# Attention scores in single banks: one exponential per tile of keys, and a fourth side bank

## The chip, the cores and the metric

One core of a Trainium2 chip runs the whole program in one launch. The metric is the device time of one execution in microseconds (us). The core's engines each work through their own list of instructions in order: PE (matmul, with PEld for its weight loads), ACT (activations), DVE (vector), POOL (general purpose) and SP (issues DMAs). They meet through semaphores. PE writes to a memory of its own, PS in the code, with eight banks; a bank holds 512 fp32 numbers for each of 128 partitions.

## The reference

Two sublayers over x of 2 x 2048 tokens x 256, each modulated by a small conditioning vector c. What matters here is the attention of the second one:

```python
nx = _rmsnorm(X, g1)
Q = (nx @ Wq.T).reshape(B, S, H, dk).transpose(0, 2, 1, 3)     # H = 4, dk = 64, S = 2048
Kc = nx @ Wkc.T
Vc = nx @ Wvc.T
scores = jnp.einsum('bhsd,btd->bhst', Q, Kc) * scale
attn = jax.nn.softmax(scores, axis=-1)
out = jnp.einsum('bhst,btd->bhsd', attn, Vc)
```

Before it stand a layer norm, a projection and a softmax over heads; after it an output projection, routing of each token to 2 of 8 experts, the experts and a shared expert (gated feed-forward), and the combination.

## The kernel before

The program has three parts: FRONT (everything up to the queries, keys and values), the attention loop, and a tail with the experts. Each engine runs `run(work, todo)` over lists of named jobs, which were laid out by hand (FRONT) or by rules that spread them evenly (`loop_order`, `tail_order`); a job does on each engine what that engine has to do in it, and on the others nothing.

**The attention loop** has 256 steps, gs = 0 to 255. A step is one of 8 (batch, head) pairs bh, one of 4 blocks of 512 queries qb, and one of 8 pairs of key tiles kp (2 x 128 keys). Eight steps make a block. Four things are done for each step, on different engines and at different times:

- `qk(gs)` on PE: four matmuls of 512 columns, two tiles of keys, each with a high part (KA, L1748) and a low part (KB, L1751) that are added up in the same bank. They fill two neighbouring banks, 0 and 1 or 2 and 3 in turn.
- `exp(gs)` on ACT: one exponential over both banks, 128x1024, into PT (L777), then a rounded copy PH (L780). PT, PH and PL have four slots.
- `low(gs)` on DVE: PL = PT - PH (L1190), the part that rounding lost.
- `av(gs, n)` on PE: for each of the two tiles of keys three matmuls into bank 4 (L1766, L1767, L1768), which add up over the 16 tiles of a block. After the block's last one `o_out` on ACT copies bank 4 out to OZ (L789), and the first product of the next block waits for that copy (semaphore "o"). POOL then takes OZ through a chain of small DMAs to get the reciprocal of the sums.

Each step's time is cut into parts 0, 1 and 2 (and part 3, which stands before part 0 and is used only in the last step of a bh). On PE step gs issues the scores of step gs + 1 and the products of step gs - 2:

```python
for part in range(3):
    if part == 0 and gs + 1 < NGS:
        run(work, LOOP[gs, 3])
        qk(gs + 1)
    if part and gs >= 2:
        av(gs - 2, part - 1)
    run(work, LOOP[gs, part])
```

ACT runs `exp(gs + 1)` in part 0 and `o_out(gs - 2)` at the start of part 2. DVE runs `low(gs)` between parts 0 and 1.

**Side jobs** fill the parts. The largest is `max_mm`: row maxima for the softmax of a later block need their own scores, 512 matmuls of 128x512 on PE (L1716), each reduced on DVE (L1161), 16 per block. `q_mm` (L1702) makes queries of later heads, with copies on ACT (`qst`, L760, and L768) and DVE (`q_lo`). `nx_turn`, `k_mm` and `v_mm` make the other batch's keys and values, `proj` (L1729) is the output projection, `norm` and `norm_root` (L797, L803) are for the later router, and the last 32 steps hold routing and scatter for the experts. Every side job that writes PS takes the next bank of a ring, in the order of the program: `banks.add(job, [5, 6, 7])`. `bank(...)` makes PE wait until the job that last held this bank has been read out, by ACT or by DVE.

Of the kernel before, what the change touches and what calls it, by code (L numbers as in the profile page):

```python
# [6 lines left out]
ACT = mybir.ActivationFunctionType  # L7
# [5 lines left out]
P = 128  # L13
# [11 lines left out]
NSTEP = 32  # L25
NGS = 8 * NSTEP
# [224 lines left out]
def run(work, todo):  # L251
    for name, *args in todo:
        if name in work:
            work[name](*args)
# [8 lines left out]
def _build(nc, ctx, I, out):  # L263
    named = {}

    def sem(name):
        if name not in named:
            named[name] = ctx.enter_context(nc.semaphore(name))
        return named[name]

    def sb(name, shape, dt=F32, c=None):
        return (c or ctx).enter_context(nc.sbuf_tensor(name, shape, dt))
# [3 lines left out]
    PS = ctx.enter_context(nc.psum_tensor("PS", [P, 8, 512], F32))  # L276
# [115 lines left out]
    with ExitStack() as c:  # L392
        PT = sb("PT", [P, 4, 1024], c=c)
# [7 lines left out]
    QA = [Q01[0][:, :], Q01[1][:, :], QA2[:, :]]  # L401
    QB = [Q01[2][:, :], Q01[3][:, :], QB2[:, :]]
    KA, KB = [KA0[:, :], KA1[:, :]], [KB0[:, :], KB1[:, :]]
# [22 lines left out]
    banks = Banks()  # L426
# [3 lines left out]
    for gs in range(NGS):  # L430
        for part in (3, 0, 1, 2):
            for job in LOOP[gs, part]:
                banks.add(job, [5, 6, 7])
    loop = dict(banks.count, pe=banks.n)
    banks.turn = 0
    for s in range(-2, NTL + 3):
# [8 lines left out]
    def pe_of(w, key):  # L445

        w.wait_ge(sem("pe_use"), banks.pe[key])

    def front_done(w):
        w.wait_ge(sem("pe_use"), front["pe"])  # L450
        w.wait_ge(sem("act_out"), front["a"])
        w.wait_ge(sem("dve_out"), front["v"])
        w.wait_ge(sem("h2"), 8)
        w.wait_ge(sem("x2"), 8)
        w.wait_ge(sem("ql"), 8)
        w.wait_ge(sem("qd"), 8)
        w.wait_ge(sem("kb"), 4)
        w.wait_ge(sem("xp"), 8)
        w.wait_ge(sem("dotg"), 16)
        w.wait_ge(sem("d_spill0"), 16)  # L460
        w.wait_ge(sem("d_spill1"), 16)
        w.wait_ge(sem("d_gbs"), 16)
# [10 lines left out]

    def experts_free(w):

        w.wait_ge(sem("qk"), NGS)

    def q_free(w, bh):
        if bh < 2:
            pe_of(w, ("oproj", 1, 7, 0))  # L480
        elif bh == 2:
            front_done(w)
        else:
            w.wait_ge(sem("qk"), NSTEP * (bh - 2))

    def k_free(w, b):
        if b == 0:
# [21 lines left out]

    def keys_free(w):  # L510

        w.wait_ge(sem("qk"), 4 * NSTEP)
        pe_of(w, ("max_mm", 3, 3, 3, 3, 0))

    def scattered(b, r):
# [131 lines left out]
    def _(act):  # L647
        w = Once(act)
# [119 lines left out]
                act.activation(QA[bh % 3][r, cols], qst[r, :], ACT.Copy).then_inc(sem("qh"), 1)  # L768

        def exp(gs):  # L770
            bk = 2 * (gs % 2)
            w.wait_ge(sem("qk"), gs + 1)
            if gs == 0:
                front_done(w)
            if gs >= 4:
                w.wait_ge(sem("av"), 2 * (gs - 3))
            act.activation(PT[:, gs % 4, :], PS[:, bk:bk + 2, :].rearrange("p a n -> p (a n)"), ACT.Exp,  # L777
                           scale=0.125).then_inc(sem("pt"), 1)
            w.wait_ge(sem("pt"), gs + 1)
            act.activation(PH[:, gs % 4, :], PT[:, gs % 4, :], ACT.Copy).then_inc(sem("pt_h"), 1)  # L780

        def o_out(gs):
# [802 lines left out]
    def _(pe):  # L1585
        w = Once(pe)
# [119 lines left out]
        def q_dup(bh, c):  # L1706

            w.wait_ge(sem("qd"), 8 * (bh // 2) + 2 * c + bh % 2 + 1)
# [20 lines left out]
            pe.matmul(PS[:, k, 0:256], O[:, i * P:i * P + P], woa[:, pair % 2, :], start=True,  # L1729
                      stop=True).then_inc(sem("pe_use"), 1)  # L1730

        def qk(gs):

            bh, i = divmod(gs, NSTEP)
            b, qs = bh // 4, bh % 3
            qb, kp = divmod(i, 8)
            bk, qcols = 2 * (gs % 2), slice(qb * 512, qb * 512 + 512)
            w.wait_ge(sem("d_m"), 16 * (4 * bh + qb + 1))
            q_dup(bh, qb)
            w.wait_ge(sem("ql"), 8 * (bh // 2) + 2 * qb + bh % 2 + 1)  # L1740
            out_of(w, ("k_mm", b, kp // 2, 0))
            w.wait_ge(sem("kb"), 4 * b + kp // 2 + 1)
            w.wait_ge(sem("neg"), b + 1)
            if gs >= 2:
                w.wait_ge(sem("pt"), gs - 1)
            for n in range(2):
                k0 = (2 * kp + n) * P
                pe.matmul(PS[:, bk + n, :], KA[b][:, k0:k0 + P], QA[qs][:, qcols], start=True, stop=False)  # L1748
            for n in range(2):
                k0 = (2 * kp + n) * P  # L1750
                mm = pe.matmul(PS[:, bk + n, :], KB[b][0:65, k0:k0 + P], QB[qs][0:65, qcols], start=False, stop=True)  # L1751
            mm.then_inc(sem("qk"), 1)

        def av(gs, n):

# [97 lines left out]
                "rl_turn": rl_turn, "rl_mm": rl_mm, "count": count}  # L1853
        run(work, FRONT)
        front_done(w)
        qk(0)
        for gs in range(NGS):
            for part in range(3):
                if part == 0 and gs + 1 < NGS:
                    run(work, LOOP[gs, 3])  # L1860
                    qk(gs + 1)
                if part and gs >= 2:
                    av(gs - 2, part - 1)
                run(work, LOOP[gs, part])
        for gs in range(NGS - 2, NGS):
            av(gs, 0)
            av(gs, 1)
        w.wait_ge(sem("pt"), NGS)
        w.wait_ge(sem("o"), 32)
        w.wait_ge(sem("act_out"), loop["a"])  # L1870
        w.wait_ge(sem("dve_out"), loop["v"])
# [53 lines left out]
```

## Time and profile before

| | |
|---|---|
| time, median of 3 runs | 1437.05 us (1436.15 to 1437.35) |
| the profiled execution: its own time | 1436.41 us |
| its span in the profile | 1434.5 us |
| PE busy | 1270.5 us (89% of the span) |
| DVE busy | 1089.7 us (76%) |
| ACT busy | 892.1 us (62%) |
| the stretch of the attention loop that the rows below look at | 257 to 1036 us of the span; its last steps end near 1075 us |

The profile's page gives busy times, the span in 40 slices, the chain of waits and the costliest groups of instructions. A matmul's row shows about 0.4 us, but matmuls overlap in the pipeline: where PE does not wait, the next one of 512 columns starts 0.23 us after the last. So PE counts as busy also in pauses that are shorter than the overlap, and order and spacing have to be read from the timeline.

### The profile page before, as it was taken

The numbers are of one execution on the slowest core, as the hardware profiler recorded it, in microseconds if no ns is written. First come the engines' busy times: TensorE is split into PE (matmuls) and PEld (weight loads), VectorE is DVE, ScalarE is ACT, GpSimd is POOL, SyncE is SP. The second block draws the span as 40 slices with busy tenths as digits, with TensorE's granted clock in tenths as the row PEclk, the third lists the DMA queues.
The fourth block names the chain that finished last, engine by engine and source line by source line (L and its number), as shares of the span: only waits on it lengthen the run. The fifth ranks groups of instructions, "written<-read, shape, count | busy, mean of one in ns | idle before, by whom it ended". The sixth has DMA issues, their size and how long they took to land.

```text
span 1434.5 us, 18743 instructions
## 1 busy us (share of the span) xinstructions
PE 1270.5 (89%) x5896; PEld 905.9 (63%) x5896; DVE 1089.7 (76%) x2076; ACT 892.1 (62%) x1450; POOL 350.4 (24%) x381
## 2 busy tenths in 40 slices
PE   4777676899999999999998999999877799999994
PEld 2334544566666666676765666766545687887783
DVE  4957877687988877888878888888833757547688
ACT  2355565577776766776787766676636656555451
POOL 0443340112211121110212211111272001723346
PEclk9889787899999999999999999999979899999998
DMA  5000017100000000000000001000020423655644
GB/s 199 8 1 37 23 59 242 56 8 6 4 9 4 5 9 4 5 9 4 9 4 4 9 4 56 9 5 28 22 84 27 145 63 106 200 155 171 184 128 147
DMA packets 61376, 80.71 MB, mean 56 GB/s; under 512 B 12002, under 2 KB 51682, under 8 KB 61026
## 3 DMA queue, kind: packets, MB, share of 16 engines
q1 hardware_dynamic: 36384, 46.81, 10.1%
q0 software_dynamic: 10752, 21.18, 5.4%
q10 hardware_dynamic: 14146, 11.52, 2.4%
q8 instruction: 52, 0.85, 0.3%
q14 instruction: 42, 0.34, 0.1%
HBM read 41.79 MB, written 37.62 MB: 55 GB/s over the span
## 4 chain that ended last, share of the span: by engine, by line
PE 57%; DVE 10%; POOL 5%; DMA 4%; ACT 3%; issue 3%; SPq 2%; POOLq 0%; ACTq 0%; DVEq 0%
PE PS L1819 8%; PE PS L1748 7%; PE PS L1751 7%; PE PS L1766 6%; PE PS L1768 6%; PE PS L1767 6%; PE PS L1716 6%; PE PS L1845 4%; DVE mx L1161 4%; DVE PL L1190 3%; POOL xbuf L1540 2%; SPq L633 2%; POOL y L1552 2%; PE PS L1803 1%; PE PS L1702 1%
## 5 line engine op out<-in xcount | busy, mean ns | idle before, releaser
L777 ACT ACTIVATE PT<-PS 128x1024 f32<-128x1024 f32 x256 | 262.4, 1025 | 211.0 <-PE PS L1751 210.8
L1161 DVE TENSOR_REDUCE mx<-PS 128x1 f32<-128x512 f32 x512 | 336.9, 683 | 67.2 <-PE PS L1716 66.1
L1190 DVE TENSOR_TENSOR PL<-PT,PH 128x1024 fp32r<-128x1024 f32 x256 | 317.8, 1242 | 13.2 <-ACT PH L780 12.8
L780 ACT ACTIVATE PH<-PT 128x1024 fp32r<-128x1024 f32 x256 | 271.6, 1061 | 8.1
L1766 PE MATMUL PS<-PH,VH 128*65 128x512 f32 x512 | 215.1, 420 | 10.6 <-DVE PL L1190 8.8
L1768 PE MATMUL PS<-PL,VH 128*65 128x512 f32 x512 | 205.0, 400 | 0.0
L1767 PE MATMUL PS<-PH,VL 128*65 128x512 f32 x512 | 204.4, 399 | 0.0
L1716 PE MATMUL PS<-KA,Q 128*128 128x512 f32 x384 | 156.5, 418 | 9.6 <-DVE mx L1161 6.0
L1748 PE MATMUL PS<-Q,KA 128*128 128x512 f32 x384 | 129.2, 418 | 13.0 <-DMA Q<-mT 11.1
L1751 PE MATMUL PS<-Q,KB 65*128 65x512 f32 x384 | 123.0, 402 | 0.0
L1515 POOL DMA_DIRECT2D z_scratch<-OZ x32 | 17.6, 550 | 386.5 <-ACT OZ L789 386.5
L1716 PEld LDWEIGHTS PS<-KA,Q 128*128 128x128 f32 x384 | 74.7, 195 | 49.9 <-DVE mx L1161 15.9
L1767 PEld LDWEIGHTS PS<-PH,VL 128*65 128x65 f32 x512 | 70.7, 138 | 50.0 <-issue 5.4
L1768 PEld LDWEIGHTS PS<-PL,VH 128*65 128x65 f32 x512 | 70.5, 138 | 50.2 <-issue 2.4
L1540 POOL DMA_INDIRECT xbuf<-nxT,slot x64 | 65.0, 1015 | 141.5 <-DVE nxT L1348 123.8
L1766 PEld LDWEIGHTS PS<-PH,VH 128*65 128x65 f32 x512 | 70.8, 138 | 41.3 <-issue 16.3
L1370 DVE TENSOR_TENSOR xl<-PS,xh 128x256 fp32r<-128x256 f32 x110 | 46.3, 421 | 60.0 <-ACT xh L860 59.6
L1748 PEld LDWEIGHTS PS<-Q,KA 128*128 128x128 f32 x384 | 70.7, 193 | 33.3 <-DMA Q<-mT 11.5
L1552 POOL DMA_INDIRECT y<-ybuf,slot x64 | 62.3, 973 | 99.3 <-DVE X L1402 52.5
L1751 PEld LDWEIGHTS PS<-Q,KB 65*128 65x128 f32 x384 | 74.0, 193 | 17.9
L867 ACT ACTIVATE sg<-PS 128x256 f32<-128x256 f32 x110 | 42.2, 383 | 61.0 <-PE PS L1819 60.6
L1377 DVE TENSOR_TENSOR hg<-PS,sg 128x256 f32<-128x256 f32 x110 | 46.3, 421 | 41.8 <-ACT sg L867 41.7
(243 smaller groups left out, 2502.6 us busy)
## 6 DMA issues: line engine op xcount, KB each, us to landing
xbuf<-xT SPq DMA_DIRECT2D x26, 384.0 KB, 4.9
xg<-xbuf SPq DMA_DIRECT2D x78, 128.0 KB, 2.3
ybuf<-yo ACTq DMA_DIRECT2D x78, 128.0 KB
nxT<-in_wexp SPq DMA_DIRECT2D x9, 768.0 KB, 4.4
x<-in_x SPq DMA_DIRECT2D x8, 512.0 KB, 11.9
x_scratch<-x SPq DMA_DIRECT2D x2, 2048.0 KB, 7.3
Z<-z_scratch POOLq DMA_DIRECT2D x32, 128.0 KB, 3.1
nxT<-x_scratch SPq DMA_DIRECT2D x32, 128.0 KB
```

Source lines behind the costliest of these rows:

```text
L777: act.activation(PT[:, gs % 4, :], PS[:, bk:bk + 2, :].rearrange("p a n -> p (a n)"), ACT.Exp, scale=0.125).then_inc(sem("pt"), 1)
L780: act.activation(PH[:, gs % 4, :], PT[:, gs % 4, :], ACT.Copy).then_inc(sem("pt_h"), 1)
L1161: dve.tensor_reduce(mx[:, qb % 2, i, c:c + 1], PS[:, k, :], AX, ALU.max).then_inc(sem("dve_out"), 1)
L1190: dve.tensor_tensor(PL[:, gs % 4, :], PT[:, gs % 4, :], phf[:, gs % 4, :], ALU.subtract).then_inc(sem("pl"), 1)
L1540: pool.indirect_dma_start(out=xbuf[b], out_offset=bass.IndirectOffsetOnAxis(ap=slot[:, b, j, i:i + 1], axis=0), in_=sx[:, r, :], in_offset ...
L1716: pe.matmul(PS[:, k, :], QA[bh % 3][:, q0:q0 + P], KA[b][:, c * 512:c * 512 + 512], start=True, stop=True).then_inc(sem("pe_use"), 1)
L1748: pe.matmul(PS[:, bk + n, :], KA[b][:, k0:k0 + P], QA[qs][:, qcols], start=True, stop=False)
L1751: mm = pe.matmul(PS[:, bk + n, :], KB[b][0:65, k0:k0 + P], QB[qs][0:65, qcols], start=False, stop=True)
L1766: pe.matmul(PS[0:65, 4, :], VH[:, t, :], PH[:, h, c], start=first, stop=False)
L1767: pe.matmul(PS[0:65, 4, :], VL[:, t, :], PH[:, h, c], start=False, stop=False)
L1768: pe.matmul(PS[0:65, 4, :], VH[:, t, :], PL[:, h, c], start=False, stop=last).then_inc(sem("av"), 1)
L1819: mm = pe.matmul(PS[:, k, :], a[:, r, dc, :], wsel(part, ex, dc, 0, 512), start=(n == 0), stop=(n == 5))
```

## The change

The four score banks become three single ones (0, 1, 2) in a ring, and bank 3 joins the ring of the side jobs, which is then 3, 5, 6, 7. `qk` now does one tile of keys, two matmuls into one bank: tile u = 2 gs + n goes to bank u mod 3, and waits for the exponential of tile u - 3. The exponential of a step becomes two of 512 columns, each waiting for its own tile; the rounded copy stays one of 1024 columns and waits for both. On PE the first tile of step gs + 1 stays at the start of part 0; the second goes to the end of part 1, behind the first three products. Waits that count steps by "qk" or "pt" count twice as far.

```diff
@@ -430,7 +430,7 @@
     for gs in range(NGS):
         for part in (3, 0, 1, 2):
             for job in LOOP[gs, part]:
-                banks.add(job, [5, 6, 7])
+                banks.add(job, [3, 5, 6, 7])
     loop = dict(banks.count, pe=banks.n)
     banks.turn = 0
     for s in range(-2, NTL + 3):
@@ -473,7 +473,7 @@
 
     def experts_free(w):
 
-        w.wait_ge(sem("qk"), NGS)
+        w.wait_ge(sem("qk"), 2 * NGS)
 
     def q_free(w, bh):
         if bh < 2:
@@ -481,7 +481,7 @@
         elif bh == 2:
             front_done(w)
         else:
-            w.wait_ge(sem("qk"), NSTEP * (bh - 2))
+            w.wait_ge(sem("qk"), 2 * NSTEP * (bh - 2))
 
     def k_free(w, b):
         if b == 0:
@@ -509,7 +509,7 @@
 
     def keys_free(w):
 
-        w.wait_ge(sem("qk"), 4 * NSTEP)
+        w.wait_ge(sem("qk"), 8 * NSTEP)
         pe_of(w, ("max_mm", 3, 3, 3, 3, 0))
 
     def scattered(b, r):
@@ -768,15 +768,16 @@
                 act.activation(QA[bh % 3][r, cols], qst[r, :], ACT.Copy).then_inc(sem("qh"), 1)
 
         def exp(gs):
-            bk = 2 * (gs % 2)
-            w.wait_ge(sem("qk"), gs + 1)
             if gs == 0:
                 front_done(w)
             if gs >= 4:
                 w.wait_ge(sem("av"), 2 * (gs - 3))
-            act.activation(PT[:, gs % 4, :], PS[:, bk:bk + 2, :].rearrange("p a n -> p (a n)"), ACT.Exp,
-                           scale=0.125).then_inc(sem("pt"), 1)
-            w.wait_ge(sem("pt"), gs + 1)
+            for n in range(2):
+                u = 2 * gs + n
+                w.wait_ge(sem("qk"), u + 1)
+                act.activation(PT[:, gs % 4, n * 512:n * 512 + 512], PS[:, u % 3, :], ACT.Exp,
+                               scale=0.125).then_inc(sem("pt"), 1)
+            w.wait_ge(sem("pt"), 2 * gs + 2)
             act.activation(PH[:, gs % 4, :], PT[:, gs % 4, :], ACT.Copy).then_inc(sem("pt_h"), 1)
 
         def o_out(gs):
@@ -1729,27 +1730,23 @@
             pe.matmul(PS[:, k, 0:256], O[:, i * P:i * P + P], woa[:, pair % 2, :], start=True,
                       stop=True).then_inc(sem("pe_use"), 1)
 
-        def qk(gs):
+        def qk(gs, n):
 
             bh, i = divmod(gs, NSTEP)
             b, qs = bh // 4, bh % 3
             qb, kp = divmod(i, 8)
-            bk, qcols = 2 * (gs % 2), slice(qb * 512, qb * 512 + 512)
+            u, qcols, k0 = 2 * gs + n, slice(qb * 512, qb * 512 + 512), (2 * kp + n) * P
             w.wait_ge(sem("d_m"), 16 * (4 * bh + qb + 1))
             q_dup(bh, qb)
             w.wait_ge(sem("ql"), 8 * (bh // 2) + 2 * qb + bh % 2 + 1)
             out_of(w, ("k_mm", b, kp // 2, 0))
             w.wait_ge(sem("kb"), 4 * b + kp // 2 + 1)
             w.wait_ge(sem("neg"), b + 1)
-            if gs >= 2:
-                w.wait_ge(sem("pt"), gs - 1)
-            for n in range(2):
-                k0 = (2 * kp + n) * P
-                pe.matmul(PS[:, bk + n, :], KA[b][:, k0:k0 + P], QA[qs][:, qcols], start=True, stop=False)
-            for n in range(2):
-                k0 = (2 * kp + n) * P
-                mm = pe.matmul(PS[:, bk + n, :], KB[b][0:65, k0:k0 + P], QB[qs][0:65, qcols], start=False, stop=True)
-            mm.then_inc(sem("qk"), 1)
+            if u >= 3:
+                w.wait_ge(sem("pt"), u - 2)
+            pe.matmul(PS[:, u % 3, :], KA[b][:, k0:k0 + P], QA[qs][:, qcols], start=True, stop=False)
+            pe.matmul(PS[:, u % 3, :], KB[b][0:65, k0:k0 + P], QB[qs][0:65, qcols], start=False,
+                      stop=True).then_inc(sem("qk"), 1)
 
         def av(gs, n):
 
@@ -1853,19 +1850,22 @@
                 "rl_turn": rl_turn, "rl_mm": rl_mm, "count": count}
         run(work, FRONT)
         front_done(w)
-        qk(0)
+        qk(0, 0)
+        qk(0, 1)
         for gs in range(NGS):
             for part in range(3):
                 if part == 0 and gs + 1 < NGS:
                     run(work, LOOP[gs, 3])
-                    qk(gs + 1)
+                    qk(gs + 1, 0)
                 if part and gs >= 2:
                     av(gs - 2, part - 1)
                 run(work, LOOP[gs, part])
+                if part == 1 and gs + 1 < NGS:
+                    qk(gs + 1, 1)
         for gs in range(NGS - 2, NGS):
             av(gs, 0)
             av(gs, 1)
-        w.wait_ge(sem("pt"), NGS)
+        w.wait_ge(sem("pt"), 2 * NGS)
         w.wait_ge(sem("o"), 32)
         w.wait_ge(sem("act_out"), loop["a"])
         w.wait_ge(sem("dve_out"), loop["v"])
```

**On PE, the last step of one block and the start of the next** (`L1748`/`L1751` scores, `L1716` side maxima, `L1766` to `L1768` products into bank 4; the product that waits for "o" is the next block's first). Before:

```order
L1716 MATMUL PS<-KA,Q 128x512 [waits dve_out]
L1766 MATMUL PS<-PH,VH 65x512
L1767 MATMUL PS<-PH,VL 65x512
L1768 MATMUL PS<-PL,VH 65x512
L1716 MATMUL PS<-KA,Q 128x512 [waits dve_out]
L1748 MATMUL PS<-Q,KA 128x512 [waits pt]
L1748 MATMUL PS<-Q,KA 128x512
L1751 MATMUL PS<-Q,KB 128x512 x2
L1716 MATMUL PS<-KA,Q 128x512 [waits dve_out]
L1766 MATMUL PS<-PH,VH 65x512 [waits o,pl,pt_h]
```

and now (scores are L1747 and L1748, maxima L1717, products L1763 to L1765):

```order
L1717 MATMUL PS<-KA,Q 128x512 [waits dve_out]
L1747 MATMUL PS<-Q,KA 128x512 [waits pt]
L1748 MATMUL PS<-Q,KB 128x512
L1763 MATMUL PS<-PH,VH 65x512
L1764 MATMUL PS<-PH,VL 65x512
L1765 MATMUL PS<-PL,VH 65x512
L1717 MATMUL PS<-KA,Q 128x512 [waits dve_out]
L1747 MATMUL PS<-Q,KA 128x512 [waits pt]
L1748 MATMUL PS<-Q,KB 128x512
L1717 MATMUL PS<-KA,Q 128x512 [waits dve_out]
L1763 MATMUL PS<-PH,VH 65x512 [waits o,pl,pt_h]
```

Between the last product of one block and the first of the next stood four score matmuls; now there are two, and the other two of a step stand ahead of its last three products.

**On ACT, at the same place** (the exponential, the rounded copy, and the copy of bank 4 to OZ). Before:

```order
L777 ACTIVATE PT<-PS 128x1024 [waits av,qk]
L780 ACTIVATE PH<-PT 128x1024 [waits pt]
L789 ACTIVATE OZ<-PS 65x512 [waits on,av]
L777 ACTIVATE PT<-PS 128x1024 [waits qk]
L780 ACTIVATE PH<-PT 128x1024 [waits pt]
```

and now:

```order
L778 ACTIVATE PT<-PS 128x512 [waits qk,av]
L778 ACTIVATE PT<-PS 128x512 [waits qk]
L781 ACTIVATE PH<-PT 128x1024 [waits pt]
L790 ACTIVATE OZ<-PS 65x512 [waits on,av]
```

The copy to OZ still stands behind the rounded copy, and that one now stands behind a second wait for scores.

## Rows read from the trace of the kernel before

**Rows 1.** The page: busy time of each engine
```profile
PE 1270.5 (89%) x5896; PEld 905.9 (63%) x5896; DVE 1089.7 (76%) x2076; ACT 892.1 (62%) x1450; POOL 350.4 (24%) x381
```

**Rows 2.** Windows: stretch, its length, busy PE, PEld, DVE, ACT, POOL; granted clock, DMA
```profile
257.00:1036.00 779.00, 759.30 (x3281) 520.05 (x3282) 663.09 (x991) 562.19 (x628) 134.55 (x180) 0.99 0.04 10
733.00:757.00 24.00, 20.25 (x82) 12.57 (x81) 15.29 (x24) 23.13 (x46) 2.91 (x4) 1.00 0.02 6
757.30:760.60 3.30, 3.30 (x9) 2.36 (x8) 2.07 (x3) 2.29 (x5) 0.54 (x1) 0.50 0.00 0
```

**Rows 3.** Waits of PE, 262 to 1036 us: total us, times, longest
```profile
PE PS L1716 <- DVE mx L1161: 6.4, 11, 1.3
PE PS L1702 <- DVE mx L1161: 4.5, 4, 1.2
PE PS L1716 <- ACT qst L760: 2.4, 1, 2.4
PE PS L1766 <- ACT OZ L789: 1.7, 2, 0.9
PE PS L1676 <- DVE mx L1161: 1.5, 3, 0.9
```

**Rows 4.** Timeline of PE at one change of blocks: start, length, instruction
```profile
287.77 0.63 PE L1748 MATMUL PS<-Q,KA 128*128 128x512 f32 x2
288.23 0.63 PE L1751 MATMUL PS<-Q,KB 65*128 65x512 f32 x2
...
288.93 0.39 PE L1766 MATMUL PS<-PH,VH 128*65 128x512 f32 x1
...
290.31 0.39 PE L1768 MATMUL PS<-PL,VH 128*65 128x512 f32 x1
...
291.94 0.40 PE L1766 MATMUL PS<-PH,VH 128*65 128x512 f32 x1
```

**Rows 5.** Timeline of ACT at the same place
```profile
288.90 1.03 ACT L777 ACTIVATE PT<-PS 128x1024 f32<-128x1024 f32 x1 [0.68 <-PE PS L1751]
289.95 1.06 ACT L780 ACTIVATE PH<-PT 128x1024 fp32r<-128x1024 f32 x1
290.92 0.57 ACT L789 ACTIVATE OZ<-PS 65x512 f32<-65x512 f32 x1
```

**Rows 6.** Timelines of PE and DVE before a query matmul
```profile
366.25 0.39 PE L1716 MATMUL PS<-KA,Q 128*128 128x512 f32 x1
367.87 1.13 PE L1702 MATMUL PS<-nxT,wqp 128*128 128x512 f32 x2 [1.23 <-DVE mx L1161]
...
362.68 1.87 DVE L1161 TENSOR_REDUCE mx<-PS 128x1 f32<-128x512 f32 x3
```

**Rows 7.** Timeline of PE where four maxima follow one another
```profile
536.81 0.61 PE L1716 MATMUL PS<-KA,Q 128*128 128x512 f32 x2
538.55 1.10 PE L1716 MATMUL PS<-KA,Q 128*128 128x512 f32 x2 [1.13 <-DVE mx L1161]
```

**Rows 8.** Timelines of ACT and PE, the same at two other changes of blocks
```profile
864.35 0.58 ACT L789 ACTIVATE OZ<-PS 65x512 f32<-65x512 f32 x1
...
865.35 0.39 PE L1766 MATMUL PS<-PH,VH 128*65 128x512 f32 x1
...
339.84 0.59 ACT L789 ACTIVATE OZ<-PS 65x512 f32<-65x512 f32 x1
...
340.58 0.41 PE L1766 MATMUL PS<-PH,VH 128*65 128x512 f32 x1 [0.84 <-ACT OZ L789]
```

**Rows 9.** Groups by line (L760: 257 to 1036 us): busy us, mean ns, idle before
```profile
L777 ACT ACTIVATE PT<-PS 128x1024 f32<-128x1024 f32 x256 | 262.4, 1025 | 211.0 <-PE PS L1751 210.8
L1190 DVE TENSOR_TENSOR PL<-PT,PH 128x1024 fp32r<-128x1024 f32 x256 | 317.8, 1242 | 13.2 <-ACT PH L780 12.8
...
L760 ACT ACTIVATE qst<-PS 128x512 f32<-128x512 f32 x12 | 7.1, 593 | 11.5 <-PE PS L1702 11.5
```

**Rows 10.** Waits of DVE, 262 to 1036 us
```profile
DVE PL L1190 <- ACT PH L780: 8.1, 16, 1.5
```

## The prediction

> **What bounds the kernel now.** Start with the page: PE is busy for 89% of the span, the others far less [rows 1]. Then look at the stretch that the change touches. From 257 to 1036 us PE is busy for 759.3 of 779 us, DVE for 663.1 and ACT for 562.2 [rows 2]. So the loop goes at PE's pace. The change gives PE the same matmuls, so all it can do is take away pauses of PE or add some.
>
> The waits of PE name the pauses [rows 3]. The side ring of three banks accounts for most: PE waits for a row maximum on DVE (mx) for 6.4 + 4.5 + 1.5 us, and for the ACT copy qst once for 2.4 us. Two waits of 0.9 us are for OZ, the copy that frees bank 4. No row names the exponential: PE never waits for a score bank.
>
> Last comes the timeline [rows 4, 5], the view that decides here, since it shows how much room a wait has that costs nothing yet. The step from 287.77 us has twelve 512-column matmuls, which start 0.23 us apart.
>
> **The side ring of four banks (a gain).** The waits for mx come to 12.4 us in 18 times. Matmuls show 0.39 us but start every 0.23, so each pause is 0.16 us longer than its row: 2.9 us more, and two small mx waits outside these rows add about 1. That is 16 us, of which about 1.4 (the longest of the waits, 1.3 us) lies between 733 and 757 us, where ACT sets the pace (below). So 15 us is the most that the ring can give back. How much of it comes? Before the query matmul the pause is 367.87 - 366.25 - 0.23 = 1.4 us; its bank's maximum was queued behind other DVE work, while the maximum one bank further back belongs to the group done by 364.55 [rows 6]. Such a pause goes whole. Where four maxima follow one another the third waits 1.5 us (538.55 - 536.81 - 0.23), and with one more bank the fourth waits instead, for what the third waited for: about 0.6 of the loss goes [rows 7]. There are more single pauses than bursts. I take 11 of the 15 us, with 5 and 15 as ends.
>
> **The drain of bank 4 (a loss).** Between two blocks PE can't start the new block's first product until ACT has copied bank 4 to OZ. Before: the last product starts at 290.31, OZ ends at 290.92 + 0.57 = 291.49, and the product comes at 291.94 [rows 4, 5]. At its tightest PE follows OZ by 0.15 us (339.84 + 0.59 = 340.43, then 340.58) [rows 8], so the room is 291.94 - 291.49 - 0.15 = 0.30 us. Now put the same step in the new order, with a start every 0.23 us:
>
> - First tile's scores at 287.77 and 288.00, a maximum, three products, a maximum, then the second tile's scores at 289.40 and 289.63. They end at 290.03; before, all scores ended at 288.86. ACT is 1.17 us later with its last exponential, which is shorter: 0.59 us instead of 1.03 [rows 9]. The rounded copy ends 0.74 us later, and OZ is queued right behind it: it ends at about 292.23, and PE could follow at 292.38.
> - PE's turn comes earlier, as only two score matmuls stand between the blocks: 291.94 - 0.46 = 291.48.
>
> The pause is 292.38 - 291.48 = 0.90 us, which is a shift of 1.2 less the room of 0.30. The gap between OZ's end and the next product is 0.43 to 0.48 us at 16 of the 31 changes of block, as at 864.35 + 0.58 = 864.93 and 865.35 [rows 8]: 16 x 0.9 = 14.4. At four it is 0.14 to 0.15, as at 340.58, with no room: 4 x 1.2 = 4.8. At two it is 0.40 (1.9 together), at two 0.60 and 0.65 (1.4), at one 0.91 (0.4). At the six others PE itself was late and has 1.15 to 2.75 us: 0.2 in all. The sum is 23 us; I take 2 off for the last changes, beyond 960 us, where routing on DVE and POOL's chain also hold PE. So +21, with ends of +8 (if ACT runs ahead more than I see) and +26.
>
> **Where ACT is full.** From 733 to 757 us ACT is busy for 23.13 of 24 us: norms and two table loads lie there [rows 2]. Two exponentials of 593 ns instead of one of 1025 [rows 9] add 0.16 us a step, over eight steps 1.3; and PE may now run only one and a half steps ahead of ACT instead of two. Together +2, ends 0 and +5. Elsewhere the 0.16 x 256 = 41 us of ACT work lies in its idle time (217 us in the stretch), and this cover holds as long as PE's step is longer than ACT's 0.59 + 0.59 + 1.06 us plus a side job.
>
> **DVE.** `low` waits for the rounded copy, which comes 0.74 us later. In the stretch it waits for that copy 16 times, 8.1 us in all [rows 10]; these waits grow by 0.74 us each, 12 us, and a few steps that now just miss waiting join them: some 14 us more of idle DVE. What is queued behind it are maxima, which PE waits for. Against that, each pause at bank 4 lets DVE catch up by 0.9 us, so fewer waits for mx are left. I let these cancel and put the net at -2, ends -4 and +10.
>
> **More increments.** A matmul with an increment is followed as closely as one without: from L1768 at 290.31, which has one, to the product at 291.94 are seven starts of 0.233 us each, and four of the seven follow one [rows 4]. So the 256 added increments are costed at nothing. The Trainium skill, "TensorE: Matmul & The Clock Gate", section "The cost: per-tile semaphore tail", says that increments serialize at about 26 ns each; if that lay on PE's path here the sum would be some 7 us higher (an estimate from that page). This trace speaks against it.
>
> **The sum.** -11 + 21 + 2 - 2 = +10 us on the profiled execution's 1436.4, which is 0.6 below the median of the runs: 1446.4, and on the median's footing 1447.
>
> **Rivals.**
>
> *Faster.* The ring gives back all 15 us, and the wait at bank 4 grows by little: if OZ kept its old time in spite of the later copy, only the 0.46 us of PE's earlier turn would count, less the room of 0.30, or 16 x 0.16 + 4 x 0.46 = 4 us. Then -15 + 4 + 2 = -9: 1428. For it: OZ depends on products alone, not on scores. Against it: ACT takes its list in order, and the new order has OZ behind the copy. It decides above a room of 1.2 us; the rows show 0.30. Chance 13%.
>
> *No change.* The drain costs half, 0.45 us at a change of blocks: -11 + 10.5 + 2 - 2 = -0.5, or 1437. Chance 10% within the 0.2% (2.9 us) that a measurement of this kernel can tell from nothing.
>
> *The clock.* After the one pause of 2.5 us (the wait for qst [rows 3], plus 0.16), at 753 us, the granted clock was 0.50 from 757.3 to 760.6, the 1.2 GHz level, and 1.00 (2.4 GHz) around it [rows 2]; pauses of up to 1.5 us [rows 6, 7] left it full, and the mean over the stretch is 0.99. If pauses of 0.9 us at each block brought such a drop, each would cost 3.3 / 2 = 1.7 us, 25 of them 42: 1489. The Trainium skill's same page, section "A second HAM failure mode: psum-queue depth-cycling", tells of a kernel whose small idle gaps between groups of matmuls made the clock go up and down; here the trace agrees only after the long pause. Chance 3%.
>
> *DVE becomes the bound.* Its 14 us of added idle all reach PE and the ring returns only 5: -5 + 21 + 5 + 14 = +35, or 1472. For it: where maxima run, two or three to a step, DVE has 1.24 + 2.4 x 0.62 = 2.7 us of work [rows 6, 9] in PE's 2.9. Against it: DVE mostly starts `low` well behind the copy. Chance 9%.
>
> **Chances and range.** The forecast, slower by 4 to 20 us, has 65%. Slower in all 77%, same 10%, faster 13%. The range leaves out the faster rival's far half and the two dear ones: 1433 to 1461.
>
> **What would show it.** In the new profile: waits of L1763 for OZ, about 25 times 0.7 us (the row shows 0.16 less than the pause), 15 to 19 us in all, in place of 1.7; waits for mx down to a third; OZ's end some 1.9 us after the last product's start instead of 1.2; the clock full from 262 to 1036 us but for one short stretch; the tail after the loop as long as before. I would be wrong if OZ ran ahead of the copy's delay, or if waits for mx stayed where they are.

## The result, and the profile after

The changed kernel takes 1453.1 us (median of 4 runs, 1451.3 to 1456.9) against 1436.6 us for the kernel before on the same chip (1434.5 to 1437.4). The ratio is 1.011, with a 95% interval of 1.009 to 1.013: slower by 16.5 us, where 10 were forecast.

The page of the profiled execution (own time 1453.7, span 1451.8), the rows that answer to [rows 1, 9]:

```profile
PE 1274.5 (88%) x5896; PEld 908.7 (63%) x5896; DVE 1089.6 (75%) x2076; ACT 910.3 (63%) x1706; POOL 357.8 (25%) x381
...
L1191 DVE TENSOR_TENSOR PL<-PT,PH 128x1024 fp32r<-128x1024 f32 x256 | 313.9, 1226 | 27.0 <-ACT PH L781 25.7
L778 ACT ACTIVATE PT<-PS 128x512 f32<-128x512 f32 x512 | 300.6, 592 | 233.9 <-PE PS L1748 231.2
```

PE's work is what it was. ACT has 256 instructions more; an exponential of 512 columns takes 592 ns. DVE's wait for the rounded copy has doubled, from 12.8 to 25.7 us.

The waits of PE over the same part of the loop, now 262 to 1052 us; these answer to [rows 3]:

```profile
PE PS L1763 <- ACT OZ L790: 20.3, 24, 2.0
PE PS L1717 <- DVE mx L1162: 2.6, 3, 1.3
PE PS L1723 <- DVE m L1166: 2.2, 3, 1.2
PE PS L1747 <- ACT PT L778: 2.1, 2, 1.5
PE PS L1763 <- DVE PL L1191: 2.0, 1, 2.0
PE PS L1717 <- ACT qst L760: 1.1, 1, 1.1
```

One kind of wait has been traded for another. The waits for maxima have gone from 6.4 + 4.5 + 1.5 to 2.6 us, and the wait for OZ, twice 0.9 us before, now comes at 24 changes of block. The 2.0 us under PL on DVE are a 25th: at that change OZ ends 0.14 us before the product, as at the others. The step of [rows 4, 5] in the new order, PE and then ACT (start, length, instruction):

```profile
289.77 0.39 PE L1747 MATMUL PS<-Q,KA 128*128 128x512 f32 x1
290.00 0.40 PE L1748 MATMUL PS<-Q,KB 65*128 65x512 f32 x1
...
291.40 0.40 PE L1747 MATMUL PS<-Q,KA 128*128 128x512 f32 x1
291.63 0.40 PE L1748 MATMUL PS<-Q,KB 65*128 65x512 f32 x1
...
292.33 0.39 PE L1765 MATMUL PS<-PL,VH 128*65 128x512 f32 x1
...
293.26 0.39 PE L1717 MATMUL PS<-KA,Q 128*128 128x512 f32 x1
294.38 0.42 PE L1763 MATMUL PS<-PH,VH 128*65 128x512 f32 x1 [0.73 <-ACT OZ L790]
```

```profile
292.06 0.60 ACT L778 ACTIVATE PT<-PS 128x512 f32<-128x512 f32 x1 [0.86 <-PE PS L1748]
292.69 1.06 ACT L781 ACTIVATE PH<-PT 128x1024 fp32r<-128x1024 f32 x1
293.66 0.58 ACT L790 ACTIVATE OZ<-PS 65x512 f32<-65x512 f32 x1
```

The last product starts at 292.33 and its row ends at 292.72, but OZ starts only at 293.66, when ACT has done the second exponential and the rounded copy. PE's pause is 294.38 - 293.26 - 0.23 = 0.89 us; the prediction had 0.90. At three changes, the 4th, 12th and 20th, two copies of queries (L768) stand ahead of OZ as well, and there the pause is 2.2 us. Each of these three was followed by a stretch of 3.3 to 3.4 us in which the granted clock was 0.50, the 1.2 GHz level. First the pause and two matmuls in the stretch behind it, then the three stretches (granted clock in the third column from the right):

```profile
344.31 0.42 PE L1763 MATMUL PS<-PH,VH 128*65 128x512 f32 x1 [2.03 <-ACT OZ L790]
...
346.24 0.63 PE L1763 MATMUL PS<-PH,VH 128*65 128x512 f32 x1
346.67 0.63 PE L1764 MATMUL PS<-PH,VL 128*65 128x512 f32 x1
```

```profile
345.10:348.50 3.40, 3.40 (x10) 2.33 (x9) 1.05 (x2) 1.66 (x2) 1.78 (x3) 0.50 0.03 1
560.20:563.50 3.30, 3.30 (x10) 2.01 (x9) 0.80 (x2) 2.25 (x3) 1.78 (x3) 0.50 0.03 1
775.20:778.50 3.30, 3.30 (x9) 2.16 (x8) 0.85 (x2) 1.65 (x2) 1.78 (x3) 0.50 0.02 1
```

In the first of them nine starts, from 345.03 to 348.67, take 3.64 us, where nine at 0.23 take 2.1: a stretch costs PE about 1.6 us. The kernel before had one such stretch in this part of the loop [rows 2].

Comparing the start of each block's first product in the two traces shows where the time goes. From the first change of block to the second and from there to the third the changed kernel falls behind by 0.94 us (269.5, 291.9, 314.4 before; 271.0, 294.4, 317.8 after). At the start of the 28th change it is 16.7 us behind (967.1 and 983.9), and from there to the end of the span it is 17.3. The loop from first to last L1768 (now L1765) shows it in one row each, before and then after, as loads of its weights:

```profile
L1768 PEld LDWEIGHTS PS<-PL,VH x512: 134/135/228, 233.2 to 1080.2; 128*65 128x65 f32 x171
```

```profile
L1765 PEld LDWEIGHTS PS<-PL,VH x512: 134/135/228, 233.8 to 1098.1; 128*65 128x65 f32 x171
```

That is 847.0 and 864.3 us: all of the loss is in the loop (whose last product comes at 1080 us before, not near 1075 as the table of the time before has it). The experiments below read the same row.

### The profile page after: what moved, and what is told of

Its sections match the earlier page's. It is cut to its first block, busy times and chain, and to the rows that moved or that the text cites. A ratio compares the mean times of both kernels' runs of the same rounds, so it can differ in the third digit from the quotient of the medians.

```text
span 1451.8 us, 19000 instructions
## 1 busy us (share of the span) xinstructions
PE 1274.5 (88%) x5896; PEld 908.7 (63%) x5896; DVE 1089.6 (75%) x2076; ACT 910.3 (63%) x1706; POOL 357.8 (25%) x381
## 4 chain that ended last, share of the span: by engine, by line
PE 58%; DVE 6%; POOL 5%; ACT 5%; issue 4%; DMA 3%; SPq 2%; POOLq 0%; ACTq 0%; DVEq 0%
PE PS L1816 8%; PE PS L1763 7%; PE PS L1747 7%; PE PS L1748 6%; PE PS L1765 6%; PE PS L1764 6%; PE PS L1717 6%; PE PS L1842 4%; POOL xbuf L1541 2%; SPq L633 2%; DVE mx L1162 2%; POOL y L1553 2%; DVE PL L1191 2%; PE PS L1730 1%; PE PS L1800 1%
## 5 line engine op out<-in xcount | busy, mean ns | idle before, releaser
L778 ACT ACTIVATE PT<-PS 128x512 f32<-128x512 f32 x512 | 300.6, 592 | 233.9 <-PE PS L1748 231.2
L1191 DVE TENSOR_TENSOR PL<-PT,PH 128x1024 fp32r<-128x1024 f32 x256 | 313.9, 1226 | 27.0 <-ACT PH L781 25.7
L1763 PE MATMUL PS<-PH,VH 128*65 128x512 f32 x512 | 214.9, 420 | 32.5 <-ACT OZ L790 21.1
L1765 PE MATMUL PS<-PL,VH 128*65 128x512 f32 x512 | 204.6, 400 | 0.0
L1747 PE MATMUL PS<-Q,KA 128*128 128x512 f32 x384 | 162.6, 423 | 14.0 <-DMA Q<-mT 11.6
L1717 PE MATMUL PS<-KA,Q 128*128 128x512 f32 x384 | 155.7, 419 | 5.3 <-POOL Q L1509 2.9
L1748 PE MATMUL PS<-Q,KB 65*128 65x512 f32 x384 | 155.1, 404 | 0.0
L1763 PEld LDWEIGHTS PS<-PH,VH 128*65 128x65 f32 x512 | 71.7, 140 | 67.9 <-issue 23.9
L1765 PEld LDWEIGHTS PS<-PL,VH 128*65 128x65 f32 x512 | 70.7, 138 | 50.6 <-issue 2.9
L1717 PEld LDWEIGHTS PS<-KA,Q 128*128 128x128 f32 x384 | 75.1, 196 | 42.7 <-DVE mx L1162 6.8
L1747 PEld LDWEIGHTS PS<-Q,KA 128*128 128x128 f32 x384 | 74.1, 193 | 39.4 <-DMA Q<-mT 12.0
L1748 PEld LDWEIGHTS PS<-Q,KB 65*128 65x128 f32 x384 | 74.3, 194 | 15.6 <-issue 0.7
```

Of the source, the lines that this page charges most:

```text
L778: act.activation(PT[:, gs % 4, n * 512:n * 512 + 512], PS[:, u % 3, :], ACT.Exp, scale=0.125).then_inc(sem("pt"), 1)
L1191: dve.tensor_tensor(PL[:, gs % 4, :], PT[:, gs % 4, :], phf[:, gs % 4, :], ALU.subtract).then_inc(sem("pl"), 1)
L1717: pe.matmul(PS[:, k, :], QA[bh % 3][:, q0:q0 + P], KA[b][:, c * 512:c * 512 + 512], start=True, stop=True).then_inc(sem("pe_use"), 1)
L1747: pe.matmul(PS[:, u % 3, :], KA[b][:, k0:k0 + P], QA[qs][:, qcols], start=True, stop=False)
L1748: pe.matmul(PS[:, u % 3, :], KB[b][0:65, k0:k0 + P], QB[qs][0:65, qcols], start=False, stop=True).then_inc(sem("qk"), 1)
L1763: pe.matmul(PS[0:65, 4, :], VH[:, t, :], PH[:, h, c], start=first, stop=False)
```

## The experiments

The twelve runs are variants of the changed kernel (one is of the kernel before). First the four that change one part each; they ran beside the kernel before at 1436.1 us.

**OZ ahead of the rounded copy** (`e1_drain_first`). Where a block ends, ACT copies bank 4 out behind the second exponential.

```diff
-        def exp(gs):
+        def exp(gs, drain=None):
...
                 act.activation(PT[:, gs % 4, n * 512:n * 512 + 512], PS[:, u % 3, :], ACT.Exp,
                                scale=0.125).then_inc(sem("pt"), 1)
+            if drain is not None:
+                o_out(drain)
             w.wait_ge(sem("pt"), 2 * gs + 2)
...
-                    exp(gs + 1)
-                if part == 2 and gs >= 2:
+                    exp(gs + 1, gs - 2 if gs >= 2 else None)
+                if part == 2 and gs == NGS - 1:
                     o_out(gs - 2)
```

Expected:

> The changed kernel with one thing moved: at the end of a block ACT copies bank 4 to OZ behind the second exponential and ahead of the rounded copy. If the loss is the copy to OZ that stands behind the later rounded copy (20.3 us of waits in 24 times, each 0.16 us longer in truth, so 24 us), then these waits go almost whole and the time is 1453 - 24 = 1429 us, below the kernel before (the side ring's gain is left over, less a little for the rounded copies that come 0.6 us later once per block). The rival, that the later second tile of scores and what DVE loses by it make the loss, leaves it at 1445 to 1453. A second rival, that PE is simply slower in the alternated order, gives the same.

Measured: 1425.8 us, ratio 0.992 (0.991 to 0.994). The waits for OZ are gone, the 25th under PL among them, and the others stand much as they were (the wait for O on POOL comes in the changed kernel too, 5.6 us, behind 1052 us):

```profile
PE PS L1732 <- POOL O L1535: 5.6, 1, 5.6
PE PS L1765 <- DVE PL L1193: 3.0, 4, 2.1
PE PS L1719 <- DVE mx L1164: 2.6, 3, 1.3
```

The trace also has no stretch at half clock between 275 and 1020 us (granted clock 1.00). So the place of OZ in ACT's list is worth 27 us, the whole loss and more, and the kernel that is left is 10 us faster than the one before. The rivals, that the second tile's place or DVE made the loss, fall for four side banks.

**Three side banks in the changed kernel** (`e2_three_side`).

```diff
-                banks.add(job, [3, 5, 6, 7])
+                banks.add(job, [5, 6, 7])
```

> The changed kernel with the side ring of 5, 6, 7 as before, bank 3 unused. If the fourth side bank gives back the waits for maxima (13.3 us of rows before, about 3 now), this is 7 to 14 us slower than the changed kernel, 1460 to 1467 us, and waits for mx are back at 10 us or more. The rival, that the pauses at bank 4 already let DVE catch up and the fourth bank is worth nothing, gives 1453 within 2 us.

Measured: 1471.7 us, ratio 1.025 (1.023 to 1.026): 18.6 us slower than the changed kernel, more than expected. The waits for OZ stay, and the waits that come back are not all for DVE:

```profile
PE PS L1763 <- ACT OZ L790: 21.9, 24, 2.0
PE PS L1717 <- DVE mx L1162: 5.8, 8, 1.5
PE PS L1703 <- DVE mx L1162: 4.7, 3, 1.6
PE PS L1717 <- ACT qst L760: 4.2, 6, 2.0
PE PS L1717 <- ACT xT L814: 2.9, 4, 0.9
PE PS L1717 <- DVE KA L1141: 2.5, 3, 0.9
```

Waits for qst, xT and KA, banks that ACT reads or that DVE reads after ACT, were there once in the kernel before (qst, 2.4 us). The pauses of 2.2 us stand at the 4th, 12th and 20th change here too, but no stretch at half clock follows them in this trace (granted clock 1.00 from 274 to 1036 us): such a pause need not bring one.

**Both tiles of scores together** (`e3_scores_together`).

```diff
                     qk(gs + 1, 0)
+                    qk(gs + 1, 1)
                 if part and gs >= 2:
                     av(gs - 2, part - 1)
                 run(work, LOOP[gs, part])
-                if part == 1 and gs + 1 < NGS:
-                    qk(gs + 1, 1)
```

> The changed kernel with both tiles of scores of a step at the start of part 0 again, one behind the other; single banks, two exponentials and four side banks stay. If the place of the second tile makes the loss, the waits for OZ fall to 2 us or less (ACT is done with the rounded copy 0.3 us earlier than in the kernel before) and the ring's gain is left: 1424 to 1431 us. The rival, that three score banks are too few without the alternation, shows waits of L1747 for the exponential (PT) and 1440 us or more.

Measured: 1426.9 us, ratio 0.994 (0.992 to 0.995). The wait for OZ is back at 1.8 us in 3 times. PE waits for an exponential for 4.7 us in 2 times, one of them 4.1 us: that is the rival's wait, but only where ACT is full.

```profile
PE PS L1747 <- ACT PT L778: 4.7, 2, 4.1
PE PS L1763 <- ACT OZ L790: 1.8, 3, 0.8
```

**The rounded copy split** (`e4_copy_split`).

```diff
                                scale=0.125).then_inc(sem("pt"), 1)
-            w.wait_ge(sem("pt"), 2 * gs + 2)
-            act.activation(PH[:, gs % 4, :], PT[:, gs % 4, :], ACT.Copy).then_inc(sem("pt_h"), 1)
+                w.wait_ge(sem("pt"), u + 1)
+                cp = act.activation(PH[:, gs % 4, n * 512:n * 512 + 512], PT[:, gs % 4, n * 512:n * 512 + 512], ACT.Copy)
+            cp.then_inc(sem("pt_h"), 1)
```

> The changed kernel with the rounded copy split too: the first half stands behind the first exponential, in what is now idle time of ACT, and only the second half (about 0.6 us instead of 1.06) stands between the second exponential and OZ. By the theory OZ ends 0.45 us earlier, each wait for OZ shrinks from 0.85 to 0.4 us, and the time falls by 10 to 13 us to 1441. The rival, that ACT has no time to spare (0.2 us more of work per step), gives 1453 or more.

Measured: 1437.7 us, ratio 1.001 (1.000 to 1.002): 15 us less than the changed kernel. The wait for OZ shrinks but stays at every block:

```profile
PE PS L1764 <- ACT OZ L791: 12.3, 24, 1.6
```

That is 8 us less in the same 24 waits, 0.33 us each where 0.45 were expected (each half of the copy takes 0.63 us, more than half of 1.06). The three longest pauses are 1.77 us now instead of 2.2, and no stretch at half clock follows them: three times 1.6, or 5 us more of the gain. The theory holds in place and sign, and the rival falls: ACT had the 0.2 us per step to spare.

These four left a question. Three side banks cost 18.6 us in the alternated order, and the prediction allowed at most 15. Four more runs, beside the kernel before at 1436.6 us:

**Together, three side banks** (`e5_together_three`): the edits of `e3_scores_together` and `e2_three_side`.

> Both tiles of scores at the start of part 0, single banks, two exponentials, but a side ring of three banks (5, 6, 7). With four side banks this was 1426.9 us. The prediction's figure for the ring was 11 us (ends 5 and 15), so 1438 us with waits for mx back at 13 us: the time of the kernel before, if splitting the exponential costs nothing by itself. The rival: the ring is worth 18 us, as it was in the alternated order (1471.7 against 1453.1), which gives 1445 us.

Measured: 1436.9 us, ratio 1.000 (0.998 to 1.002). Here the fourth bank is worth 10 us, as the prediction had it, and single banks with two exponentials cost nothing by themselves. The waits for mx come to 9.4 us in the rows, less than the 13 expected.

**Alternated, OZ first, three side banks** (`e6_drain_first_three`): the edits of `e1_drain_first` and `e2_three_side`.

> The alternated order with the copy to OZ ahead of the rounded copy, and a side ring of three banks. It shows what alternation costs apart from the drain and without the fourth bank to hide it. Theory: rounded copies 0.74 us later make DVE idle longer, and PE waits for maxima; with three banks that reaches PE, 1471.7 - 27 = 1445 us or about 9 over the kernel before, the ring being worth 19. Rival: all of the alternation's cost was the drain, and this is the kernel before within 3 us, the ring being worth 11.

Measured: 1452.9 us, ratio 1.011 (1.008 to 1.013). Neither number was right: 1445 took over the 27 us of `e1_drain_first`, but with three side banks moving OZ is worth 19 (1471.7 to 1452.9), and the rival's 1437 is far off. With three side banks alternation costs 16 us that have nothing to do with bank 4, and the fourth side bank is worth 27 us here. Its waits:

```profile
PE PS L1719 <- DVE mx L1164: 8.1, 9, 1.8
PE PS L1705 <- DVE mx L1164: 6.3, 6, 1.6
PE PS L1719 <- ACT qst L760: 4.3, 6, 2.0
PE PS L1719 <- ACT xT L816: 3.2, 4, 1.2
PE PS L1719 <- DVE KA L1143: 2.5, 3, 0.9
```

**OZ first and the copy split** (`e7_drain_first_split`): the edits of `e1_drain_first` and `e4_copy_split`, with OZ between the second exponential and the second half of the copy.

> The alternated order with the copy to OZ ahead of the second half of the rounded copy, which is split as well; four side banks. If the later rounded copy still costs PE anything through DVE, this is 2 to 4 us below 1425.8; if not, it is the same within 1.5 us, or 1 to 3 us above for the 0.2 us of ACT work more in each step where ACT is full.

Measured: 1421.7 us, ratio 0.989 (0.987 to 0.991), the fastest of this group and 4 us under `e1_drain_first` (0.992, 0.991 to 0.994). The two intervals touch, and the loops differ by 3 us (832.4 and 835.3), so the gain is likely and not settled. DVE's wait for the rounded copy falls from 22.3 to 16.2 us over the span:

```profile
L1194 DVE TENSOR_TENSOR PL<-PT,PH 128x1024 fp32r<-128x1024 f32 x256 | 314.4, 1229 | 16.9 <-ACT PH L783 16.2
```

**The kernel before, OZ first** (`e8_before_drain_first`): the edit of `e1_drain_first` on the kernel before.

> The kernel before with one edit: the copy to OZ ahead of the rounded copy. There was room of 0.30 us at this wait and only 1.7 us of rows, so the theory says 1434 to 1437 us, the same or up to 2 us faster: the edit is worth 27 us only where the change has used the room up. Rival: the earlier drain is worth several us by itself (POOL's chain on OZ starts earlier), 1430 us or less.

Measured: 1438.2 us, ratio 1.001 (1.000 to 1.003). Where there was room at this wait, moving OZ gains nothing; it is worth 27 us only behind the change.

The last four ask what the 16 us of alternation are. They ran beside the kernel before at 1462.3 us, so only their ratios and their loops are compared with the runs above; the section on the hardware says where that chip's extra time lies.

**ACT's side jobs in PE's order** (`e10_act_order_three`), on `e6_drain_first_three`: the side jobs of parts 0 and 1 stand between the two exponentials.

```diff
             for n in range(2):
+                if n:
+                    run(work, between)
                 u = 2 * gs + n
...
-                    exp(gs + 1, gs - 2 if gs >= 2 else None)
+                    exp(gs + 1, gs - 2 if gs >= 2 else None, LOOP[gs, 0] + LOOP[gs, 1])
...
-                run(work, LOOP[gs, part])
+                if part == 2 or gs + 1 == NGS:
+                    run(work, LOOP[gs, part])
```

> The alternated order, copy to OZ ahead of the rounded copy, three side banks (1452.9 us so far), and on ACT the side jobs of parts 0 and 1 stand between the two exponentials, in PE's order, instead of behind both exponentials and the rounded copy. Theory A: what alternation costs beyond the drain (16 us with three banks) is side banks that ACT reads late (waits for qst, xT, KA: 10 us of rows), so those rows go and the time falls by 8 to 14 us, to 1439 to 1445. Theory B: the cost is DVE waiting for the later rounded copy; then this changes little, 1450 or more, since the rounded copy comes no earlier.

Measured: ratio 0.994 (0.992 to 0.996) against 1.011 for `e6_drain_first_three`. The loops, first `e6_drain_first_three`, then this one:

```profile
L1767 PEld LDWEIGHTS PS<-PL,VH x512: 134/135/228, 235.6 to 1097.1; 128*65 128x65 f32 x171
```

```profile
L1770 PEld LDWEIGHTS PS<-PL,VH x512: 134/135/228, 237.3 to 1076.7; 128*65 128x65 f32 x171
```

861.5 and 839.4 us: 22 us for the order of ACT's side jobs alone, more than theory A asked for. PE waits no more for qst, xT or KA, and for maxima it waits less too (the wait for O on POOL is not new, it lay behind 1052 us in the slower kernel). These rows, with 0.16 us for each wait, give some 16 of the 22 us; the rest is open:

```profile
PE PS L1722 <- DVE mx L1167: 6.2, 7, 2.2
PE PS L1735 <- POOL O L1538: 5.2, 1, 5.2
PE PS L1708 <- DVE mx L1167: 4.5, 6, 1.0
```

Theory B falls: DVE waits for the rounded copy as long as it did, first `e6_drain_first_three`, then this one.

```profile
DVE PL L1193 <- ACT PH L783: 21.7, 25, 1.6
DVE PL L1196 <- ACT PH L785: 22.5, 28, 1.6
```

**The copy split, three side banks** (`e11_split_three`): `e7_drain_first_split` with the edit of `e2_three_side`.

> The same kernel of 1452.9 us with the rounded copy split in two, the first half in ACT's idle time, so that PH is complete 0.45 us earlier; ACT's side jobs stay behind it. Theory A (ACT reads side banks late): they are read 0.45 us earlier too, so a third of the cost goes, 1446 to 1450. Theory B (DVE waits for the rounded copy 0.74 us longer): more than half of the cost goes, 1440 to 1445, with the waits for mx down from 15 to 10 us and those for qst, xT, KA as before.

Measured: ratio 1.003 (1.001 to 1.005) against 1.011, about 10 us, and a loop of 852.1 us (235.2 to 1087.3) against 861.5. The waits for qst, xT and KA are 3.3, 1.7 and 1.2 us, down from 4.3, 3.2 and 2.5, and those for maxima 7.1 and 4.0, down from 8.1 and 6.3. The ratio, put on 1436.6 us, is 1441, which theory B gave; but B left the waits for qst, xT and KA as they were, and they fell from 10.0 to 6.2 us. Everything that waits behind the copy gains, so this run does not tell the theories apart; the run before it does.

**Together with all repairs** (`e9_together_best`): `e7_drain_first_split` with the edit of `e3_scores_together`.

> Both tiles of scores together, four side banks, rounded copy split, copy to OZ ahead of its second half: only the place of the second tile differs from the kernel of 1421.7 us. If alternation is worth nothing by itself, this is 1420 to 1424 us; if it spares PE waits (it gives ACT a lead between the tiles), this is 1425 or more, near the 1426.9 of the kernel with the scores together and one whole rounded copy.

Measured: ratio 0.991 (0.988 to 0.993), against 0.989 (0.987 to 0.991) alternated. The intervals overlap. The loop is 836.0 us (236.0 to 1072.0) and the alternated one 832.4 (233.1 to 1065.5), and PE waits 5.7 us for an exponential in 3 times, one of them 4.4 us, where ACT is full. Two stretches at half clock lie in this loop (746 to 749 and 992 to 995 us, granted clock 0.50), the first right behind that long wait, and none in the other; at 1.6 us each they are 3 of the 3.6 us. That alternation by itself is worth anything here is not shown.

**ACT's side jobs in PE's order, on the fastest** (`e12_act_order_split`): `e7_drain_first_split` with the edit of `e10_act_order_three`.

> The fastest so far (alternated, four side banks, split rounded copy, OZ first: 1421.7 us) with ACT's side jobs of parts 0 and 1 between the exponentials. With four side banks only 1.6 us of rows are waits for qst, so 1420 to 1422 us; more than 1423 if side jobs ahead of the second exponential hold up rounded copies.

Measured: ratio 0.991 (0.988 to 0.994), the same as `e7_drain_first_split` within the intervals; loop 830.8 us (234.5 to 1065.3). With four side banks the order of ACT's side jobs no longer matters to within 3 us or so. It has a small price too: waits for OZ come back, 3.1 us in 3 times.

## Why the prediction was right, and where its terms were off

**The mechanism was the one forecast.** The prediction said that the rounded copy would end 0.74 us later, that OZ would stand behind it, that PE would come 0.46 us earlier, and that the 0.30 us of room would turn into a pause of 0.90. The trace shows 0.89. It asked for some 25 waits for OZ of 15 to 19 us in all; there are 24 with 20.3, and the one under PL. `e1_drain_first` and `e8_before_drain_first` together show the cause: the same edit is worth 27 us behind the change and nothing ahead of it. (The step at 287.77 has thirteen matmuls, not the twelve that the prediction counted; nothing rests on that.)

**The sum, term by term.** The runs lead from the kernel before to the changed one in three steps. Single banks and a fourth side bank, scores together: 1436.1 to 1426.9, or -9, where the ring's term was -11. Alternation with OZ out of the way: 1426.9 to 1425.8, or -1, where ACT and DVE were +2 - 2. OZ behind the copy: 1425.8 to 1453.1, or +27, where the drain was +21. So most of the forecast's error is in the drain.

**The drain: forecast +21, measured 27.** Over all 31 changes of block PE's pauses add up to 27.5 us in the changed kernel and 2.8 in the one before: 24.7 more. The prediction's list of the changes came to 23, and what it took off for the last ones was a mistake, since the 28th, 29th and 31st pause for 1.2, 0.9 and 0.9 us. The 20th it had left out, as one of six where PE itself came late. PE was late there because it ran at half clock from 757.3 to 760.6 [rows 2], and the changed kernel pauses for 2.2 us at that place. At the 5th, 13th and 21st it was right that almost nothing is lost: OZ ends 0.21, 0.23 and 0.18 us ahead of the product, where 0.14 means that PE waited. The other part is the clock, which the drain's term leaves out: three stretches of 1.6 us in the changed kernel, one in the kernel before, none with OZ moved.

**The side ring: forecast -11, and its worth depends on the order.** The four kernels in which PE hardly waits for OZ (the left column ran beside the kernel before at 1436.6 us, the right one at 1436.1):

| | three side banks | four side banks |
|---|---|---|
| scores together | 1436.9 us (ratio 1.000) | 1426.9 us (0.994) |
| alternated, OZ first | 1452.9 us (1.011) | 1425.8 us (0.992) |

With the scores together the fourth bank is worth 10 us, in the middle of the forecast's 5 to 15; in the alternated order with OZ first it is worth 27, and with OZ behind the copy 18.6 (1471.7 to 1453.1).

**What the prediction did not see.** Alternation costs 16 us with three side banks and nothing with four. That the term for DVE, -2, came out well is therefore in part luck. The prediction looked for what is queued behind the second wait for scores on DVE alone (row maxima; its 14 us of added waiting for the copy are 12.7 in the trace, 8.1 to 20.8). It let them cancel against the pauses at bank 4, in which DVE catches up; but in `e1_drain_first` these pauses are gone and PE's waits for maxima are the same 2.6 us, so it is not the pauses that kept them short. And it did not look at what is queued behind that wait on ACT: the side jobs' own reads of their banks. In the new order PE issues the second tile behind the side jobs of parts 0 and 1, while ACT reads those jobs' banks only behind that tile's exponential and copy. With three banks the side job three places on then waits for the bank. `e10_act_order_three` moves only these reads and takes 22 us out of the loop. With four banks a bank comes up one side job later, and the cost is gone.

**ACT where it is full: +2 forecast.** From the 19th to the 20th change of block the lag grows by 1.3 us (729.7 and 741.9, then 760.6 and 774.2). The pause at the 20th, 2.2 us instead of 0.2, is more than that, so no cost of ACT's own shows there.

**The rivals.** The faster one needed OZ at its old time; `e1_drain_first` makes that by hand and lands at 1425.8, where that rival had put 1428. No change: the drain did not cost half. The clock: pauses of 0.9 us at each block did not bring it down, and the mean over the loop stayed 0.99.

```profile
262.00:1052.00 790.00, 757.89 (x3266) 517.62 (x3266) 659.78 (x988) 576.30 (x865) 140.35 (x179) 0.99 0.04 10
```

But the rival was not idle: the three pauses of 2.2 us were followed by 3.3 to 3.4 us at half clock each, and the sign that the prediction gave, a full clock but for one short stretch, did not hold. The Trainium skill, "TensorE: Matmul & The Clock Gate", section "A second HAM failure mode: psum-queue depth-cycling", tells of clocks that go up and down with small idle gaps between groups of matmuls; this trace agrees behind its three longest pauses only, and the trace of `e2_three_side`, with pauses as long, does not. DVE as the bound: it did not come with four banks. The 256 added increments cost nothing that can be seen: L1748 with its increment at 291.63 is followed at 291.87, 0.24 us later, so nothing like an added 26 ns lies on PE's path. (The Trainium skill, "TensorE: Matmul & The Clock Gate", section "The cost: per-tile semaphore tail", has that figure for the tail of small matmuls that are packed together, which these are not.)

The Trainium skill, "Perfetto Trace Analysis", section "Optimizing Scalar/DVE Operations", says that breaking up Scalar instructions may let work be completed sooner where that engine is not saturated but causes bubbles on others. Splitting the exponential alone did nothing (`e5_together_three`, ratio 1.000). Splitting the rounded copy, which others wait for, gave 15 us with OZ behind it, about 10 with OZ first and three side banks, and with four some 4 that the intervals do not settle.

## What to carry to other kernels

When a producer's instruction is moved later on one engine, list what stands behind its consumer in every in-order queue, and for each item who waits for it: here the copy of bank 4 and side jobs that had nothing to do with scores were held up by a wait for scores. Read the room at each such wait from the timeline (end of the releaser to start of the waiter, less the least such gap in the trace) before and after the move; 0.30 us of room against a shift of 1.2 us decided this case. A wait that is hidden behind something else, as at the 20th change behind a slow clock, comes out when that goes. Measure a buffer's worth in the order in which it will be used: one more side bank was worth 10, 19 and 27 us in three orders of the same work. When an order of one engine is changed, change the other engines' lists to follow it, or add a buffer: either one alone took away the whole side-bank loss here, and with OZ first and the copy split the same change is 1.1% faster than the kernel before.

## What the runs showed of the hardware

**The clock after a pause.** In the changed kernel three pauses of 2.2 us in a steady loop were each followed, about 1 us after PE had gone on, by 3.3 to 3.4 us at a granted clock of 0.50, which cost PE some 1.6 us each. None of its pauses of 0.9 us up to 1052 us was, and in `e2_three_side` three pauses of 2.2 us were not either.

**The stretch after the loop on another chip.** The last four kernels ran where the kernel before took 1462.3 us instead of 1436.6. No kernel has a trace on both chips, but their loops are as short as their edits ask for, and the extra lies after the loop. From the last product to the end of the span `e7_drain_first_split` takes 352.5 us (1065.5 to 1418.0) and `e12_act_order_split`, whose code is the same from there on, 379.1 us (1065.3 to 1444.4). In that stretch PE waits 19.1 us in 11 times for xl on DVE, where the other trace has 4.4 us in 10. DVE in turn stands still ahead of xl with no releaser in the profile ("issue"), which the other trace never shows:

```profile
DVE xl L1377 <- issue: 15.3, 5, 6.0
```

ACT has such idle times there too, and the clock is at half for 45 us instead of 35. Why an engine that waits for nothing visible stands still is open.
